# Second phase of a three-phase decoder layer: logits issued three slots ahead, masked minimum before the low part of the probabilities

## The reference

```python
def _L0_xattn_ref(x, mem_seq, mem_mask, rms_scale, q_w, kv_w, out_w):
    NUM_HEADS, NUM_KV, HEAD_DIM, WIDTH = (4, 1, 128, 512)
    MASK_FILL = -2.3819763e+38
    xn = _rmsnorm(x, rms_scale)
    mn = _rmsnorm(mem_seq, rms_scale)
    q = jnp.einsum('BTD,NDH->BTNH', xn, q_w)
    kv = jnp.einsum('BSD,cKDH->cBSKH', mn, kv_w)
    k, v = (kv[0], kv[1])
    q = _apply_rope(q, q_pos) * HEAD_DIM ** (-0.5)
    k = _apply_rope(k, k_pos)
    q = q.reshape(B, T, NUM_KV, G, HEAD_DIM)
    logits = jnp.einsum('BTKGH,BSKH->BKGTS', q, k)
    masked = jnp.where(mem_mask[:, None, None, None, :], logits, MASK_FILL)
    probs = jax.nn.softmax(masked, axis=-1).astype(x.dtype)
    enc = jnp.einsum('BKGTS,BSKH->BTKGH', probs, v).reshape(B, T, NUM_HEADS, HEAD_DIM)
    return jnp.einsum('BTNH,NHD->BTD', enc, out_w)
# in the layer
x = x + _L0_xattn_ref(_layernorm(x, axis=-1), ctx_1024, mask_BxS2_bk0, ...)
```

## Time and profile before

| | |
|---|---|
| Median of 3 runs | 3153.61 us (3152.2 to 3154.09) |
| Profiled execution, its own time | 3155.96 us |
| Its span, first to last instruction | 3154.2 us |
| TensorE busy | 3115.6 us, 99% |
| VectorE, ScalarE, GpSimd busy | 1778.2, 1297.7, 836.5 us |
| Mean granted clock of TensorE | 0.997 |
| Logits, first and last matmul group starts | 924.3 and 1880.0 us |

### The profile page before, as it was taken

How to read it: one execution, slowest core, us unless ns; L and a number is a source line. 1 busy time by engine, 2 the same in 40 slices (tenths; PEclk the granted TensorE clock), 3 DMA queues, 4 the chain that set the end, 5 groups by cost and what they waited for, 6 DMA issues and landing times.

```text
span 3154.2 us, 41122 instructions
## 1 busy us (share of the span) xinstructions
PE 3115.6 (99%) x15828; PEld 2630.9 (83%) x15828; DVE 1778.2 (56%) x3901; ACT 1297.7 (41%) x2475; POOL 836.5 (27%) x699
## 2 busy tenths in 40 slices
PE   8999999999989999999999989999999999999999
PEld 7888888888878888888888878888888888888887
DVE  6666665757577877777787766232232232221355
ACT  4333333333446766766666653222222212221243
POOL 0101010100146666666666650000000000000144
PEclk9999999999999999999999999999999999999999
DMA  3121121212222112211211232000001000010386
GB/s 111 41 72 50 48 73 41 81 41 94 72 99 81 57 68 78 72 69 55 95 69 55 80 103 86 27 27 27 27 31 50 27 27 27 27 54 17 122 292 227
DMA packets 118802, 220.76 MB, mean 70 GB/s; under 512 B 7504, under 2 KB 13648, under 8 KB 118608
## 3 DMA queue, kind: packets, MB, share of 16 engines
q1 hardware_dynamic: 118608, 218.14, 20.2%
HBM read 152.06 MB, written 66.06 MB: 69 GB/s over the span
## 4 chain that ended last, share of the span: by engine, by line
PE 96%; DVE 1%; ACT 1%; issue 1%; DMA 0%; POOL 0%; SPq 0%; DVEq 0%; ACTq 0%
PE c_p L132 11%; PE c_p L131 11%; PE c_p L130 11%; PE a_p L130 6%; PE a_p L132 5%; PE a_p L131 5%; PE b_n L132 5%; PE b_n L130 5%; PE b_n L131 5%; PE b_t L1580 3%; PE d_p L130 2%; PE d_p L132 2%; PE d_p L131 2%; PE a_r L130 2%; PE a_r L132 2%; PE a_r L131 2%
## 5 line engine op out<-in xcount | busy, mean ns | idle before, releaser
L1200 POOL TENSOR_SCALAR b_soft<-b_soft,b_one_in_sum 128x512 f32<-128x512 f32 x256 | 401.2, 1568 | 299.8 <-DVE b_one_in_sum L1383 299.8
L1800 ACT ACTIVATE c_gate<-c_p,c_bias 128x512 f32<-128x512 f32 x180 | 124.2, 690 | 718.3 <-PE c_p L132 718.3
L1834 DVE TENSOR_TENSOR c_gate<-c_gate,c_gate 128x512 f32<-128x512 f32 x64 | 44.3, 692 | 524.0 <-ACT c_gate L1800 524.0
L1402 DVE TENSOR_TENSOR b_p_lo<-b_t,b_p_hi 128x512 fp32r<-128x512 f32 x256 | 175.1, 684 | 159.8 <-ACT b_p_hi L1257 157.2
L1248 ACT ACTIVATE b_soft<-b_soft,b_minus_top 128x512 f32<-128x512 f32 x256 | 185.2, 723 | 180.7 <-DVE b_minus_top L1394 176.1
L344 POOL TENSOR_TENSOR kept_scale<-c_ln_ve,minus_half 128x4 f32<-128x4 f32 x16 | 16.1, 1009 | 898.5 <-DVE c_ln_ve L336 898.5
L551 ACT ACTIVATE a_elu<-a_p 128x512 f32<-128x512 f32 x128 | 76.5, 598 | 353.0 <-PE a_p L132 353.0
L344 POOL TENSOR_TENSOR a_ln_sc<-a_ln_ve,minus_half 128x4 f32<-128x4 f32 x16 | 16.3, 1017 | 695.6 <-DVE a_ln_ve L336 695.6
L1257 ACT ACTIVATE b_p_hi<-b_t 128x512 fp32r<-128x512 f32 x256 | 151.7, 592 | 108.6 <-PE b_t L1580 108.6
L1394 DVE CUSTOM_DVE_ANT_0 b_soft<-b_l,b_mask_row 128x512 f32<-128x512 f32 x256 | 175.2, 684 | 0.0
L1580 PE MATMUL b_t<-ident,b_soft 128*128 128x128 f32 x1024 | 155.7, 275 | 10.7 <-DVE b_p_lo L1402 9.6
(11 more groups left out here) (286 smaller groups left out, 9614.8 us busy)
## 6 DMA issues: line engine op xcount, KB each, us to landing
a_res<-in_x SPq DMA_DIRECT2D x16, 1024.0 KB, 5.9
x<-a_res SPq DMA_DIRECT2D x16, 1024.0 KB, 5.2
b_mem<-in_ctx SPq DMA_DIRECT2D x16, 1024.0 KB, 5.3
b_x<-x SPq DMA_DIRECT2D x16, 1024.0 KB, 5.6
b_res<-x SPq DMA_DIRECT2D x16, 1024.0 KB, 5.6
x<-b_res SPq DMA_DIRECT2D x16, 1024.0 KB, 4.5
c_x<-x SPq DMA_DIRECT2D x16, 1024.0 KB, 5.8
d_x<-x SPq DMA_DIRECT2D x16, 1024.0 KB, 6.6
```

Of the source, the lines that this page charges most:

```text
L1200: pool.tensor_scalar(soft[:, at, :], soft[:, at, :], one_in_sum[:, at:at + 1], None, ALU.mult).then_inc(p_norm.sem, p_norm.unit)
L1402: dve.tensor_tensor(part.low, pT_bank[:, :].rearrange("p (i s) -> p i s", i=T), part.high_f32(), ALU.subtract).then_inc(p_lo.sem, p_lo.unit)
L1800: act.activation(gate[j % 2][i][:, :], gating.banks[(3 * j + i) % 6][:, :], ACT.Tanh if g == "c" else ACT.Sigmoid, bias=added[:, i, j:j + ...
```

## The change

`logits` go three slots ahead in place of two: tiles 0, 1 and 2 of `new` have theirs in slots 13, 14 and 15. The two banks and the four `soft` buffers stay. The masked minimum stays two slots ahead, but on VectorE it stands before `p_low` in each slot; in slot 15 it stays behind `p_low` and `memory_low`.

```diff
-        SLOTS = 4
+        SLOTS, AHEAD = 4, 3
@@ VectorE, slot j
                         if new and j == J - 1:
                             one_over(new.b, 0)
+                        if old and j < J - 2:
+                            masked(old.b, j + 2)
+                        if new and j == J - 2:
+                            masked(new.b, 0)
                         if old and j >= 1:
                             p_low(old.b, j - 1)
                         if fin and j == 0:
                             p_low(fin.b, J - 1)
-                        if after and j == 15:
+                        if after and j == J - 1:
                             memory_low(dve, s, after, 2)
                             memory_low(dve, s, after, 3)
-                        if old and j < J - 2:
-                            masked(old.b, j + 2)
-                        if new and j >= J - 2:
-                            masked(new.b, j - J + 2)
+                        if new and j == J - 1:
+                            masked(new.b, 1)
@@ TensorE, slot j
-                        if old and j < J - 2:
-                            logits(old.b, j + 2)
-                        if s == 0 and j == J - 2:
+                        if old and j < J - AHEAD:
+                            logits(old.b, j + AHEAD)
+                        if s == 0 and j == J - AHEAD:
                             pe.wait_ge(self.a_x1.sem, self.a_x1.upto(B - 1))
-                        if new and j >= J - 2:
-                            logits(new.b, j - J + 2)
+                        if new and j >= J - AHEAD:
+                            logits(new.b, j - J + AHEAD)
```

## The result

The changed kernel takes 3163.27 us (median of 8 runs, 3162.72 to 3163.88), the kernel before 3153.61 in the same comparison (8 runs, 3151.58 to 3154.09). The ratio is 1.0031 with an interval of 1.0022 to 1.004, so the change costs 9.7 us. It is slower, as forecast; the forecast was 3164.4 us.

A forecast was written before the change was run, and what follows sets the result against it. TensorE, busy for 3115.6 of 3154.2 us, was taken to bound the kernel. Steady steps +13.3, head +0.5 and tail -3.0 gave +10.8 us on 3153.61: 3164.4 us, range 3157 to 3171.

The forecast's parts named there:

- The steady boundary: At slot 0 of 14 step boundaries, logits wait for the masked minimum of slot 15: 0.95 us each, +13.3 us.
- rival of a hidden wait: At the steady boundaries TensorE comes later or VectorE earlier, hiding the wait: same time, 3153.9 us; chance 0.11.
- Inside a step: In the other 15 of 16 slots the bank's wait is already met and the later `p_low` is covered: nothing added.
- The head: Start of step 1: tile 0 turns 1.0 to 1.5 us late, thin slots regain some: +0.5 us, -0.5 to +2.0.
- the one on the thin slots: In the head's thin slots, the earlier minimum lets ScalarE's exponential go earlier and gives back some of the late start.
- The tail: Step 16: two bare slots gain 0.66 us each, moved logits 1.42, plus some half clock: -3.0 us, -4.5 to -1.0.
- a little of the half clock back: In the tail, part of the stretch at 1.2 GHz is regained, rounding a gain of 2.7 us to 3.0.
- The clock rival: TensorE's clock falls at each of 14 boundaries, losing 3.1 us each, 43 more: 3207 us; chance 0.07.
- The sum: Steady +13.3, head +0.5, tail -3.0: +10.8 us on 3153.61, so 3164.4 us.
- some 12 us of waits: All TensorE waits in head and tail, the only places where the change can gain: 3.2 + 6.3 + 1.3 + 1.09.
- the ends win: Boundary costs under 0.1 us and ten head and tail waits shorten by 0.66 us: 8.0 us gain, 3145.6 us; chance 0.04.

The follow-up runs named there:

- the fastest kernel: Changed kernel with slot 15's masked minimum ahead of both `memory_low`, and VectorE's old order in steps holding three items: 3148.27 us, ratio 0.9985.

## Why the prediction was right, and where its sizes were off

**The steady boundary.** Forecast: 14 waits of 0.95 us, +13.3 us. The trace has 14 of 0.96 and a step of 61.66 us for 61.65. That this chain is the cause is shown by its last link alone, in four places:

| place of the boundary minimum | turn of tile 15 to logits, us over before | a step us |
|---|---|---|
| behind the low part, ahead of both `memory_low` | 0 | 60.69 (old order in full steps), 60.78 (new order) |
| between them | 0.36 | 61.06 |
| behind both (changed kernel) | 0.96 | 61.66 |
| behind the normalisation | 3.0 | 65.34 |

Since TensorE has no idle time to put a wait into, three of the four rows give 60.69 plus the wait. The rival of a hidden wait is gone: the chain hangs on the turn of tile 14, and the new order of VectorE does not advance it; with the old order the wait is the same (61.65).

**Inside a step.** Forecast: nothing, and in the changed kernel it is nothing. But where the boundary wait is absent, the new order costs 0.09 us (logits three ahead, at the turn of tile 0) to 0.11 us a step (two ahead, at the turns of tiles 13 and 14), and nothing with the old order (60.69). The forecast had named the cause, a low part one minimum further back, and had taken its cover as enough. It is enough in the changed kernel, where the boundary wait brings TensorE to the turn of tile 0 about 1 us later; without that wait the low part ends just as TensorE comes for it.

**The head.** Forecast: +0.5 us, from -0.5 to +2.0; measured -0.9, outside its bounds. The late start is there, and of the size forecast: the logits of slot 0 waited 2.31 us and tile 0 turned 0.4 us earlier by the clock of the trace, which is 1.1 later once the first phase's 1.5 is taken off. The step that failed is the one on the thin slots: they were to give back 0.5 to 1.0 us, and gave back 2.1, nearly all of it in slots 4, 5 and 6, which go from 3.28, 3.29 and 3.29 us from turn to turn to 2.81, 2.49 and 2.38. The kernel before has a loop there, from minimum to minimum 3.29 us, in which the exponential, a sum of squares (L1031, on ScalarE between the next two rows of ACT), the high copy and the low part follow one another:

```profile
944.68 0.69 DVE L1394 CUSTOM_DVE_ANT_0 b_soft<-b_l,b_mask_row 128x512 f32<-128x512 f32 x1
...
945.41 0.72 ACT L1248 ACTIVATE b_soft<-b_soft,b_minus_top 128x512 f32<-128x512 f32 x1 [0.89 <-DVE b_minus_top L1394]
...
946.75 0.58 ACT L1257 ACTIVATE b_p_hi<-b_t 128x512 fp32r<-128x512 f32 x1
...
947.36 0.69 DVE L1402 TENSOR_TENSOR b_p_lo<-b_t,b_p_hi 128x512 fp32r<-128x512 f32 x1 [0.70 <-ACT b_p_hi L1257]
...
947.97 0.69 DVE L1394 CUSTOM_DVE_ANT_0 b_soft<-b_l,b_mask_row 128x512 f32<-128x512 f32 x1
```

With the minimum first the exponential leaves this loop, as in the bare slots of the tail; the forecast had built such a loop for the tail and none for the head. The clock is not the reason, though it differs here. Busy time and granted clock of 944 to 952 us, before, after, and with three slots ahead and the old order:

```profile
944.00:952.00 8.00, 5.76 (x27) 0.79 0.01 2
```

```profile
944.00:952.00 8.00, 6.72 (x38) 1.00 0.29 88
```

```profile
944.00:952.00 8.00, 4.50 (x25) 1.00 0.00 2
```

The third kernel kept the full clock and still takes 3.28, 3.29 and 3.29 us in these slots: the loop goes through VectorE and ScalarE, and the half clock of TensorE did not lengthen it.

**The tail.** Forecast: -3.0 us, from -4.5 to -1.0; measured -4.4. Slots 11 and 12 came as forecast: 2.02 and 2.06 us for 2.02, and the loop built from three rows of other slots was right to 0.04. What was mis-sized is slots 13 and 14, for which the forecast had the 1.42 us of the logits and "a little of the half clock back". They went from 3.47 and 3.26 us to 2.07 each, 2.6 together. The kernel with three ahead and the old order, at full clock, takes 2.68 in each; so 1.4 of the 2.6 goes with the half clock and the moved logits, and 1.2 with the same shorter loop, in two slots more than were counted. Another 0.6 came in slots 1 to 3 and 9, for which the forecast said nothing, and 0.1 went the other way ahead of them. The same window that read 0.52 in the earlier trace rows, the last bare slots and what follows, now reads:

```profile
1884.00:1893.00 9.00, 6.85 (x42) 1.00 0.40 147
```

**The clock rival.** It did not happen: 1.00 from 985 to 1820. But the reason that I gave, that a lone gap between dense work leaves the clock alone, holds only for its size. Gaps that put the logits 0.96 us later left it alone, and those of 3.0 us at the same place cost 1.65 us more a step on average (the rival's price, read from the tail, was 3.1).

**The sum.** The signed errors are +0.3 (boundary), -1.4 (head) and -1.4 (tail), so the traced parts give +8.3 us; the medians say +9.7. That the total comes within 1.1 us of the forecast is in part luck: in the trace, head and tail are 2.8 us below it, and 1.4 of that is missing between the medians, which fits with the profiled execution of the kernel before having had more of the lower clock than its median one. The forecast's "some 12 us of waits" in the two ends also leaves out four rows of the view (1.1, 0.5, 0.3 and 0.8 us); no term of the sum rests on it.

**The ends alone.** The rival "the ends win" was refused for its condition, a boundary cost under 0.1 us. With that condition made true by one moved line, the ends do win: -4.0 and -5.3 us, not the 8.0 of the rival. That took 0.66 us off each of ten waits and counted no late start: in the fastest kernel's trace slots 4 to 6 of step 1 and 11 to 14 of step 16 are shorter by 0.5 to 1.4 us each, the other slots by 0.4 us at most or not at all, and the first logits of step 1 still wait 0.9 us.

## What to carry to other kernels

When a producer is sent further ahead over the same number of buffers, its release moves to a younger use of the buffer: look for the one place in the loop where that use stands last in another engine's list, above all at the seam of two steps. On an engine without idle time such a wait is paid in full, once a round (here 0.96 us, 14 times), and outweighs gains in the thin ends; moving one instruction ahead of work that nobody waits for may turn the sign. A wait too short for the view of waits can still be paid every round: the distance from the start of the releasing instruction to the start of the waiting one shows it (0.73 to 0.75 us here, where 1.37 means no wait). And an order that helps where an engine starves need not be used where it is full: each step can have its own.

## What the runs showed of the hardware

TensorE's granted clock stayed at 1.00, that is 2.4 GHz, behind 14 gaps that put the logits 0.96 us later (0.71 us idle by the view) between 60 us of dense work. It fell behind 14 gaps of 3.0 us at the same place (2.75 us idle), at the one shown to a mean of 0.63 over the next 4.6 us (between the two levels of 1.2 and 2.4 GHz, so part of that stretch ran at the lower), at a cost of 1.65 us on average on top of each gap. The Trainium skill (TensorE: Matmul & The Clock Gate, section "HAM oscillation") tells of a loop that loses the full clock in every round after its wait; the run with the late minimum agrees with that, the changed kernel does not show it at its shorter gap. One idle time between these two is in the traces: the 2.31 us ahead of the logits at the head's boundary of the changed kernel, behind 32 us in which TensorE was idle for 0.2. The clock read 1.00 in it and behind it, as in the kernel with three ahead and the old order (2.3 us):

```profile
929.11 0.50 PE L130 MATMUL b_l<-b_k_hi,b_q_hi 128*128 128x512 f32 x1 [2.31 <-DVE b_minus_top L1394]
```

```profile
900.00:985.00 85.00, 78.22 (x436) 1.00 0.22 77
```

That boundary is another place than the steady ones, so this size was not tried where the others were.

The costs of a hand-off can be read from these traces as well: from the start of the accumulator's read, which ends the minimum, to the start of the logits that wait for it took 0.14 us (1290.03 to 1290.17), and from the start of four transposes to the start of ScalarE's copy of them 0.64 us (1286.34 to 1286.98), the latter as in the kernel before (1283.94 to 1284.58).
